# One 8-head attention layer with paired 64-row score tiles and projections by group, and two 16-head layers with four 32-row strips issued together

## The reference, cut to what matters

```python
def _L0_xattn_ref(x1, x2, Wq1, Wk1, Wv1, Wk2, Wv2, Wo, bo):       # layer 1: 8 heads of 64
    q1, k1, v1 = (split_heads(x1 @ W, N1) for W in (Wq1, Wk1, Wv1))
    k2, v2 = (split_heads(x2 @ W, N2) for W in (Wk2, Wv2))
    k, v = jnp.concatenate([k1, k2], axis=1), jnp.concatenate([v1, v2], axis=1)
    attn = jax.nn.softmax(jnp.einsum('bihd,bjhd->bhij', q1, k) * scale, axis=-1)
    return jnp.einsum('bhij,bjhd->bihd', attn, v).reshape(B, N1, h * d) @ Wo + bo
def _L1_attn_ref(x, Wc_down, Wq_up, Wkv_up, Wc_proj):             # layer 3: 16 heads of 8, causal
    latent = x @ Wc_down
    att = jnp.where(causal, jnp.einsum('bthd,bsd->bhts', q, k) * scale, -jnp.inf)
    return jnp.einsum('bhts,bsd->bthd', jax.nn.softmax(att), v).reshape(B, T, C) @ Wc_proj
def _L1_xattn_ref(query, keys, values, mask, ...):                # layer 4: 16 heads of 8
    energy = jnp.where(mask[:, None, None, :] == 0, -1e20, jnp.einsum('bhqd,bhkd->bhqk', q, k))
    return (softmax(energy / sqrt(8)) @ v) @ Wo.T + bo
```

## Time and profile before

| | |
|---|---|
| median of 3 timed runs | 3980.6 us (3974.3 to 3995.62) |
| profiled execution, its own time | 3962.53 us |
| its span | 3960.0 us |
| TensorE busy | 2834.5 us (72%) |
| VectorE busy | 2306.5 us (58%) |
| ScalarE busy | 1316.6 us (33%) |
| mean DMA rate | 13 GB/s |

### The profile page before, as it was taken

One profiled execution on the slowest core, in us unless ns is written; L12 is line 12 of the kernel. 1 busy time (PEld: TensorE's weight loads), 2 busy tenths in 40 slices (PEclk: granted clock), 3 DMA queues, 4 the chain that ended last, 5 costly groups with the idle time before them and its releaser, 6 DMA issues. The chain is left out here.

```text
span 3960.0 us, 56759 instructions
## 1 busy us (share of the span) xinstructions
PE 2834.5 (72%) x20964; PEld 1688.3 (43%) x20964; DVE 2306.5 (58%) x4610; ACT 1316.6 (33%) x2011; POOL 583.3 (15%) x582
## 2 busy tenths in 40 slices
PE   4777779898867769997997897567776992233252
PEld 2544556666623324443553333435454461112241
DVE  5788833443377733333665553567776323999956
ACT  3545435555422212221333443223332330222221
POOL 1232310000000002322441000011112103000002
PEclk8888889999989969998998998778877996666665
DMA  2000000000000010000000001000001011000020
GB/s 71 1 1 1 1 9 4 6 3 3 1 0 1 0 54 1 1 1 6 10 10 1 0 0 63 22 6 6 5 3 35 24 38 40 0 0 0 0 64 21
DMA packets 40413, 51.15 MB, mean 13 GB/s; under 512 B 8843, under 2 KB 30420, under 8 KB 39060
## 3 DMA queue, kind: packets, MB, share of 16 engines
q1 hardware_dynamic: 38164, 44.19, 3.5%
q0 software_dynamic: 2048, 4.20, 0.4%
HBM read 39.19 MB, written 9.18 MB: 12 GB/s over the span
## 5 line engine op out<-in xcount | busy, mean ns | idle before, releaser
L135 POOL TENSOR_TENSOR l_rstd<-l_moments,w-1_minus_half 128x4 f32<-128x4 f32 x104 | 114.0, 1096 | 1680.9 <-DVE l_moments L129 1680.9
L917 DVE TENSOR_REDUCE l_top<-l_ring 128x8 f32<-128x1024 f32 x128 | 155.3, 1225 | 276.3 <-PE l_ring L728 276.2
L1591 PE MATMUL l_p_out<-l_hidden,w_wd 128*128 128x512 f32 x400 | 210.8, 608 | 22.8 <-DVE l_hidden L1843 11.7
L1349 DVE TENSOR_REDUCE l_top<-l_p_score 128x4 f32<-128x1024 f32 x64 | 78.3, 1224 | 249.5 <-PE l_p_score L1119 249.5
L1579 PE MATMUL l_p_gate<-l_h_t,w_wg 128*128 128x512 f32 x400 | 218.2, 629 | 7.4 <-DVE l_parts L112 7.4
L3293 PE MATMUL l_p_s<-w-1_ident,l_z 128*128 128x128 f32 x128 | 28.9, 419 | 257.4 <-ACT l_z L3340 257.4
L3033 DVE SCALAR_TENSOR_TENSOR l_mix<-l_decay,l_cb 128x1024 f32<-128x1024 f32 x128 | 163.7, 1288 | 61.2 <-ACT l_decay L2934 56.2
L141 DVE TENSOR_SCALAR l_h<-x_res,l_moments,l_rstd 128x128 f32 (+1 forms) x384 | 119.6, 374 | 110.3 <-POOL l_rstd L135 110.3
L1843 DVE TENSOR_TENSOR l_hidden<-l_act_out,l_p_spread 128x512 f32<-128x512 f32 x128 | 87.9, 687 | 127.0 <-ACT l_act_out L1659 86.2
L2934 ACT ACTIVATE l_decay<-l_p_seg 128x1024 f32<-128x1024 f32 x128 | 129.4, 1022 | 73.4 <-PE l_p_seg L2788 72.6
L3409 DVE TENSOR_TENSOR l_srt<-l_srt 128x1024 f32<-128x1024 f32 x112 | 137.3, 1226 | 3.8
(11 more groups left out here) (485 smaller groups left out, 6866.0 us busy)
## 6 DMA issues: line engine op xcount, KB each, us to landing
l_c_t<-in_ctx_t SPq DMA_DIRECT2D x24, 256.0 KB, 2.7
l_rows_in<-l_zero SPq DMA_DIRECT2D x1, 2432.0 KB
l_tile_h<-l_rows_in SPq DMA_DIRECT2D x38, 64.0 KB, 1.9
l_rows_out<-l_tile_y SPq DMA_DIRECT2D x38, 64.0 KB, 1.5
x_res<-in_x SPq DMA_DIRECT2D x1, 2048.0 KB, 7.3
w_mask<-in_mask SPq DMA_DIRECT2D x1, 2048.0 KB, 9.3
w_wg<-in_l2f_wg SPq DMA_DIRECT2D x1, 2048.0 KB
w_wu<-in_l2f_wu SPq DMA_DIRECT2D x1, 2048.0 KB
```

What stands on the lines that cost most here:

```text
L135: return nc.gpsimd.tensor_tensor(rstd[:, :], moments[:, :, 1], minus_half[:, 0:moments.shape[1]], ALU.pow)
L917: nc.vector.tensor_reduce(top[:, b % 2, half * HALF:(half + 1) * HALF, 0], s, AX.X, ALU.max)\
L1591: nc.tensor.matmul(p_out[:, :], w["wd"][:, s, :], hidden[:, s % 2, :], start=(s == 0), stop=(s == steps - 1 and kind != "top2")).then_inc( ...
```

## The change

It does four things.

In layer 1 the scores of a unit become four matmuls of 64 rows and 256 columns: the even head of a pair on rows 0 to 63 into one bank, the odd head on rows 64 to 127 into the other. The keys hold no zeros, and are copied in one instruction of 128 partitions. Queries and keys are projected for a group of four batches at once, one group ahead: twelve steps of one matmul of 512 columns, three per batch; all twelve of group 0 stand ahead of the first scores. Hardware loops become unrolled code.

In layers 3 and 4 `scores` and `turned_scores` issue all waits, then all masks, then all four strips of a kind, and count a semaphore per strip.

In layers 3 and 4 TensorE's order changes: `turned_scores(b-1)` now comes ahead of `turn_top(b)`, and the sums (L770) are split from `values` and come behind `turn_top(b)`.

In layers 3 and 4 `copy_top` moves from ScalarE to VectorE, between `reduce(b)` and `divide(b-2)`.

```diff
@@ attention16_turned, TensorE
                 def scores(b):
                     pe.wait_ge(spread_k_ready, b + 1)
-                    for half in range(2):
-                        if half == 0 and b >= 1:
-                            pe.wait_ge(top_t_ready, b)
-                        if half == 1 and b >= 2:
-                            pe.wait_ge(expd, 2 * b - 3)
-                        for i in (2 * half, 2 * half + 1):
...
-                        last.then_inc(scored, 1)
+                    if b >= 1:
+                        pe.wait_ge(top_t_ready, b)
+                    if b >= 2:
+                        pe.wait_ge(expd, 2 * b - 3)
+                    for i in range(4):
...
+                    for i in range(4):
+                        nc.tensor.matmul(score_buffer(b, i // 2)[:, i % 2, :, :], q_t[strip_of(i), q, tokens(b)],
+                                         spread_k[strip_of(i), b % 2, :, :], start=not masks, stop=True).then_inc(scored, 1)
                 def turned_scores(b):
-                    for half in range(2):
-                        if half == 0 and b >= 1:
-                            pe.wait_ge(expd, 2 * b)
-                        if half == 1 and b + 1 < NB:
-                            pe.wait_ge(reduced, 2 * b + 3)
...
+                    if b >= 1:
+                        pe.wait_ge(expd, 2 * b)
+                    if b + 1 < NB:
+                        pe.wait_ge(reduced, 2 * b + 3)
+                    if causal:
+                        for i in range(4):
+                            nc.tensor.matmul(turned_buffer(b, i // 2)[:, i % 2, :, :], causal_b[:, :],
...
@@ order of iteration b
                         values(b - 2)
                     if b < NB:
                         prepare(i + 1, 2 * u)
-                        turn_top(b)
                     if 1 <= b <= NB:
                         turned_scores(b - 1)
+                    if b < NB:
+                        turn_top(b)
+                    if b >= 2:
+                        sums(b - 2)
                     if b < NB:
                         prepare(i + 1, 2 * u + 1)
@@ VectorE
                     if b < NB:
                         reduce(b)
+                        copy_top(b)
                     if b >= 2:
                         divide(b - 2)
@@ attention8
-        q_t = L.sbuf("q_t", [T, 2, BLOCKS, T])
-        keys = L.sbuf("keys", [T, 2, BLOCKS, 2, KEYS])
+        q_t = L.sbuf("q_t", [T, 2, BLOCKS, GROUP * T])
+        keys = L.sbuf("keys", [T, 2, BLOCKS, GROUP, KEYS])
+                def project_qk(j, step):
+                    b, what = divmod(step, 3)
+                    if what == 2:
+                        pe.wait_ge(ctx_in[j % 2], 16 * (j // 2 + 1))
+                    nc.tensor.matmul(p_misc[:, :], (w["wq"], w["wk1"], w["wk2"])[what][:, b * T:(b + 1) * T],
+                                     (h_t, h_t, c_t)[what][:, j % 2, :], start=True, stop=True).then_inc(qk_done, 1)
-                    for j in range(2):
-                        b = 2 * half + j
-                        last = nc.tensor.matmul(p_score[n % 2][:, j, :], q_t[:, u % 2, b, :], keys[:, u % 2, b, :, :],
-                                                start=True, stop=True)
+                    for b in (2 * half, 2 * half + 1):
+                        for odd in range(2):
+                            rows = slice(HD8 * odd, HD8 * (odd + 1))
+                            last = nc.tensor.matmul(p_score[g % 2][:, odd, b % 2 * KEYS:(b % 2 + 1) * KEYS],
+                                                    q_t[rows, j % 2, b, u * T:(u + 1) * T], keys[rows, j % 2, b, u, :],
+                                                    start=True, stop=True)
...
+                turn_h(0)
+                pe.wait_ge(h_t_ready, 1)
+                for step in range(PER):
+                    if step:
+                        pe.wait_ge(qk_ready, step)
+                    project_qk(0, step)
...
-                        for half in range(2):
-                            part = slice(64 * half, 64 * half + 64)
-                            last = nc.scalar.copy(keys[part, u % 2, :, half, (what - 1) * T:what * T],
-                                                  p_misc[part, :].rearrange("p (b k) -> p b k", k=T))
+                        nc.scalar.copy(keys[:, j % 2, b, :, (what - 1) * T:what * T],
+                                       p_misc[:, :].rearrange("p (u k) -> p u k", k=T)).then_inc(qk_ready, 1)
-                nc.gpsimd.memset(keys[:, :, :, :, :].rearrange("p a b c d -> p (a b c d)"), 0.0).then_inc(setup, 1)
```

More of the change, by code:

```diff
@@ L1054, in attention8 @@
         dve_order = L.sem("dve_order")
[L1055 to L1066 removed]
+        UNITS8 = 2 * NB
+        head_at = lambda k: 2 * (k % 2) + k // 2
         with nc.Block() as block:
@@ L1159, in output @@
                     last.then_inc(out_done, 1)
-                def start():
-                    turn_h(0)
-                    for what in range(3):
-                        project_qk(0, 0, 0, what)
-                    pe.wait_ge(qk_ready, 3)
-                    project_v(0, 0, 0, 0)
-                    pe.wait_ge(v_ready, 1)
-                    project_v(0, 0, 0, 1)
-                    pe.wait_ge(v_ready, 2)
-                    project_qk(0, 1, 0, 0)
-                    scores(0, 0)
@@ L1229, in _ @@
-                pipelined(pe, None, start, body)
-                values(NG - 1, UNITS - 1)
-                for u in range(1, GROUP):
-                    if u > 1:
-                        pe.wait_ge(update_ready, GROUP * (NG - 1) + u)
-                        turn_out(NG - 1, u)
-                    output(NG - 1, u)
+                turn_h(0)
[4 more added lines that the diff above has]
+                    project_qk(0, step)
@@ L1237, in _ @@
+                values(UNITS8 - 1)
+                for s in range(NB - 3, NB):
+                    if s > NB - 3:
+                        pe.wait_ge(update_ready, s)
+                        turn_out(s)
+                    output(s)
             @block.scalar
@@ L1277, in copy_v, with copy_output @@
                         .then_inc(v_ready, 1)
[L1279 to L1280 removed]
+                def copy_output(s):
                     act.wait_ge(out_done, s + 1)
[L1282 removed]
+                    if s >= 1:
                         act.wait_ge(added, s)
                     nc.scalar.copy(update[:, :], p_misc[:, 0:D]).then_inc(update_ready, 1)
[L1286 to L1292 removed]
@@ L1323, in _ @@
-                pipelined(act, None, start, body)
-                for u in range(1, GROUP):
-                    if u > 1:
-                        copy_out(NG - 1, u)
-                    copy_output(NG - 1, u)
+                copy_h(0)
+                for step in range(PER):
+                    copy_qk(0, step)
+                copy_v(0, 0)
+                copy_v(0, 1)
+                copy_h(1)
+                for s in range(NB):
+                    i, u = divmod(s, GROUP)
+                    ahead = i + 1 < NG
+                    if s >= 3:
+                        copy_output(s - 3)
+                    if ahead:
+                        copy_qk(i + 1, 3 * u)
+                    exponent(2 * s)
+                    if ahead:
+                        copy_qk(i + 1, 3 * u + 1)
+                    copy_turned(2 * s)
+                    exponent(2 * s + 1)
+                    if s + 1 < NB:
+                        copy_v(s + 1, 0)
+                    if s >= 2:
+                        copy_out(s - 2)
+                    if s + 1 < NB:
+                        copy_v(s + 1, 1)
+                    copy_turned(2 * s + 1)
+                    if ahead:
+                        copy_qk(i + 1, 3 * u + 2)
+                    if u == GROUP - 1 and i + 2 < NG:
+                        copy_h(i + 2)
@@ L1329, in _ @@
+                for s in range(NB - 3, NB):
+                    if s > NB - 3:
+                        copy_out(s)
+                    copy_output(s)
             @block.vector
@@ L1388, in add_output @@
                     nc.gpsimd.tensor_tensor(x[:, s, :], x[:, s, :], update[:, :], ALU.add).then_inc(added, 1)
-                def body(i, p, last_group):
-                    if started(i):
-                        add_output(i - 1, 1)
-                        add_output(i - 1, 2)
-                    if not last_group:
-                        norm_scale(i + 1)
-                    if started(i):
-                        add_output(i - 1, 3)
-                    add_output(i, 0)
-                pipelined(pool, None, lambda: norm_scale(0), body)
-                for u in range(1, GROUP):
-                    add_output(NG - 1, u)
+                norm_scale(0)
+                norm_scale(1)
+                for s in range(NB):
+                    i, u = divmod(s, GROUP)
+                    if u == 2 and i + 2 < NG:
+                        norm_scale(i + 2)
+                    if s >= 3:
```

(3 more changed lines are left out.)

374 lines of the change are left out of this document (151 added, 223 removed).

## The result

| | before | changed |
|---|---|---|
| median of timed runs, us | 3986.1 (3974.3 to 3995.6, 4 runs) | 3889.5 (3881.0 to 3890.5, 4 runs) |
| ratio, 95% interval | | 0.9754 (0.9722 to 0.9787) |
| profiled execution, us (its span) | 3962.5 (3960.0) | 3881.0 (3879.0) |

What follows compares the result with a forecast made beforehand. TensorE alone was taken to bound layer 3, and TensorE with waits for copies layers 1 and 4. Layer 1 -50, layer 3 -78 and layer 4 +8 sum to -120 us: 3842 us profiled, 3860 timed, range 3805 to 3925.

Steps and rivals of the forecast that it cites:

- Layer 1, steady: Layer 1's batches: paired 64-row score matmuls and no wait for a key copy, 17.1 to 15.3 us each, -51 us over 28.
- rival 3: Layer 1: 64-row tiles in float32 don't pair, 42 us less gained, 3902 us; chance 0.08.
- Layer 1, start: Start of layer 1: twelve projection steps instead of four ahead of the first scores, at the low clock, +22 us.
- Layer 1, end: Last four batches of layer 1, with no projections left: -5.2 us a batch, -21 us.
- Layer 3: Four strips at once with the new order: a group of four batches 36.6 us against 46.2; the layer -78 us.
- stall of 2 us at `project`: Layer 3, batch 2 of a group: `project` waits 2 us for copy_values, which now stands behind divide.
- Layer 4: Four strips with the new order: a group 30.6 us against 29.0, slower; the layer +8 us, bounds -25 and +25.
- batch 2 of a group: Layer 4: copy_values ready 2.4 us after divide starts, project ends at 8.2, scores at 9.4; batch takes 9.6 us.
- Rival 1: No stall decides: loop hides in TensorE's work; layer 3 -102, layer 4 about -30, total 3798 us; chance 0.12.
- VectorE's order costs more: Layers 3 and 4: each group's stalls twice the forecast; layer 3 -40, layer 4 +25, total 3915 us; chance 0.12.
- Slower, by the clock: Layer 3: four-strip work with stalls drops TensorE to the low clock, +29 us a group, 4060 us; chance 0.07.
- Sum: Layers 1, 3 and 4 together: -50 - 78 + 8 = -120 us, giving 3860 us for the timed median.

Runs made afterwards that it cites:

- experiment 6: experiment 4 plus layer 1's starting projections written to four PSUM banks in turn; 0.9576 of the kernel before, median 3795.9 us, layer 1 501 us.
- experiment 1: New 8-head layer 1 alone, with the old 16-head layers 3 and 4; 0.9908 of the kernel before, median 3945.0 us, layer 3 401 us.
- experiment 5: Changed kernel with four strips together, but TensorE's order and copy_top on ScalarE as before the change; 0.9726 of the kernel before, median 3877.2 us.
- experiment 9: Changed kernel with strips of layers 3 and 4 issued in two halves again, new order kept; 1.0108 of the kernel before, median 4020.0 us.
- experiment 7: Changed kernel with layer 4's mask conversion on VectorE moved from batch 2 to batch 0 of a group; 0.9736 of the kernel before, layer 4 286 us.
- experiment 4: Changed kernel with VectorE's copy of the values moved ahead of copy_top in layers 3 and 4; 0.9637 of the kernel before, median 3837.6 us.

## Why the prediction was right, and where not

**Layer 1, steady**: right. A batch takes 15.38 us for 15.3, and a score phase 1.07 for 1.06, so that 64-row tiles pair as 32-row strips do, and rival 3 is out.

**Layer 1, start**: right in size (the first scores come 21.5 us later after the layer's start, for 22), but a fixed price it wasn't: experiment 6 shows that the waits between the steps held the clock down.

**Layer 1, end**: the term that was mis-sized. The layer gained 41 us in that profile, and 43 to 45 in most others (527 to 529 us), for 50. The last four batches were to give 5.2 us each, 21 in all. Three gave 5.0 each; the fourth gave nothing, since the old kernel too had nothing left to project there: from its first maximum to the layer's end it takes 26.4 us in experiment 1 and 26.7 before. In the changed kernel's profile it took 29.9, the clock having fallen 12 us ahead of the layer's end.

**Layer 3**: the mechanism was right. The four strips make the gain: experiment 5 has it with the old order. The stall of 2 us at `project` behind copy_values is there, 2.10 us; a group takes 37.2 for 36.6 where the clock stays up. The new order alone is a loss of 47 us (experiment 9), which the forecast never priced by itself: the strips' gain hid it. That the layer gained 86 us and not less than 78 is in part luck. From the layer's start to its first L708 it took 116 us before and 86 after, with as many matmul records. The kernel before, experiment 1 with the same old function, and the changed kernel, TensorE alone:

```profile
1436.60:1552.80 116.20, 99.65 (x585) 0.72 0.05 20
...
1392.30:1494.60 102.30, 85.43 (x585) 0.83 0.06 22
...
1397.50:1483.80 86.30, 64.93 (x586) 0.82 0.07 26
```

14 of these 30 us are the size of what an earlier rise of the clock gave the old function in experiment 1. The forecast took the clock at the start as it was and had no term for that. The five steady groups gave 43 us, for 48.

**Layer 4**: the sign was right, the size not: +29 for +8. The step that failed is batch 2 of a group, 9.6 us. The others came out nearly as worked out (batch 3 7.2 to 7.7 for 7.2, batch 0 6.0 for 5.9, batch 1 8.1 for 7.9); batch 2 took 11.2 to 12.5. A group takes 33.5 for 30.6, and of these 2.9 us:
- The conversion next to GpSimd adds 0.6. I took from the earlier trace rows the 2.4 us from divide to the last L905, in which the conversion took 0.42 us because GpSimd happened to be done; with the new order it starts 0.3 us into GpSimd's L973 and takes 1.03, and the same stretch is 3.03 us.
- The clock, which falls in that wait or within 1.6 us behind it, adds about 1.6. This is worked out from experiment 7: a group there takes 30.9 with the clock up and a wait that is 0.95 shorter (2.29 for 3.24), so some 31.9 would be left here.
- The rest, about 0.7, is spread over hand-offs and the other batches, and no run parts it.

The clock I had made a rival of its own for layer 3, priced at 29 us a group, and left out of layer 4 because four strips ran there at 1.00; those rows had only small waits.

The forecast also took the new order and the four strips in one. Experiments 5 and 9 part them: layer 4 takes 269.5 us with neither, 280 with the strips alone, 295 with the order and the moved copy_top alone, and 298 with all. So in this layer neither paid as it stood; with the copy of the values moved ahead (experiment 4) all together gain 5 us.

**Rivals.** Rival 1, that no stall decides, is out: the stall stands in both layers. The rival "VectorE's order costs more" put layer 4 at +25, and this part of it came true (+29), though not by VectorE's load: experiment 4 has the same work on VectorE in another order and layer 4 at 264, 5 less than before the change. The rule of the Trainium skill, TensorEngine Tiling (Array Packing), section PSUM Bottleneck, that emptying PSUM may bind after the tiling, isn't what bound here: VectorE was busy 103 of 167 us in the changed layer 4, and what L708 waited for was a copy out of PSUM that stood late in the queue. "Slower, by the clock" happened in small in layer 4, and in layer 3 chiefly with the order alone (experiment 9), 7 us a group where the rival had 29.

**Sum.** +9 in layer 1, -8 in layer 3, +21 in layer 4: -98 in place of -120. The other 7 of the 29 us between 3860 and 3889.5 are the reference point (the median of the kernel before was 3986 in the end, not 3981), and the rest is rounding between profile and median. The forecast's errors partly cancel: layer 3 gained 8 us more than forecast, though its groups gained less, and layers 1 and 4 missed 30 us the other way.

## What to carry to other kernels

A gain in one engine's work and a new order of the work should be priced apart: here the first hid that the second was a loss, and in layer 4 both lost. Moving one copy ahead in one queue was worth 1.2% more. Where an engine waits for another once a round, look what stands ahead of the awaited instruction in that engine's queue, and put first what is waited for. A stall on TensorE is priced with the matmuls that follow it at the lower clock, and a chain of short steps that share one PSUM bank is worth spreading over free banks even if TensorE looks 75% busy (26 us here).

## What the runs showed of the hardware

- **VectorE's int32 to bf16 `tensor_scalar` from SBUF to SBUF waits for a GpSimd operation under way.** It took 0.42 us alone, 1.00 to 1.03 us when started inside GpSimd's `tensor_tensor`; it then ended 0.27 us after GpSimd's (1905.59 and 1905.32 in the changed kernel, 1857.74 and 1857.46 in experiment 7). The Trainium skill, SBUF — State Buffer, section Who interferes with whom, has a reason for it: a VectorE operation in a mode that takes the port pair shared with GpSimd, as a `tensor_scalar` may, and a GpSimd operation exclude each other, and the one that comes second waits for the first to end. The trace agrees as to the wait; which mode VectorE was in it doesn't show.
- **TensorE's clock.** It fell to 1.2 GHz in the waits of 3.24 us at L708, or within 1.6 us behind them, in all six groups of the changed layer 4, and with waits of 2.1 to 2.3 us in some groups and not in others (one of six in the changed layer 3, four of six in experiment 7's layer 4). At the start of layer 1 it was back at 2.4 GHz within the second step without waits (experiment 6), while 14 steps of 2.07 us with 0.69 us of wait between left it at the low level. Work without waits wasn't enough everywhere: at the start of layer 3 before the change TensorE was busy 44.9 of 45.3 us at a granted clock of 0.56.
- **Two 64-row tiles run together whether the matmuls alternate between the rows or not** (1.07 us a phase in both orders).
- **An untouched layer took 4 to 7% longer on one chip than on another** (layer 8, 337 to 348 and 321 to 324 us). The other stretches that no run changed agree within about 1%, but for one that took 425 to 435 us with no clear tie to the chip.
